# Half of the turned weight rows get their remainder from Pool instead of VectorE

## The reference, cut to what matters

```python
x = fwht(x * SU_ug) / SCALE
x_up = x @ W_up.T * (Wscale_ug[:INTER] * SCALE)
x_gate = x @ W_gate.T * (Wscale_ug[INTER:] * SCALE)
x = jax.nn.silu(x_gate) * x_up
x = fwht(x * SU_dp) / SCALE
x = x @ W_down.T * (Wscale_dp * SCALE)
```

## Time and profile before

| | |
|---|---|
| median of 3 runs | 2642.16 us (2639.2 to 2642.7) |
| the profiled execution | 2643.02 us |
| its span | 2641.2 us, so 1.8 us lie around it |
| PE busy | 2573.5 us (97%) |
| DVE busy | 2243.6 us (85%) |
| POOL busy | 2044.3 us (77%) |
| ACT busy | 1815.0 us (69%) |
| granted PE clock | 0.996 of full speed |

### The profile page before, as it was taken

The page is one execution under the profiler, slowest core; times in us unless marked ns, Lnnn a source line. Parts: engine busy times, 40 slices in busy tenths (PEclk is TensorE's granted clock), DMA queues, the critical chain, the costliest instruction groups (busy, mean ns, idle before and its releaser), DMA issues.

```text
span 2641.2 us, 46296 instructions
## 1 busy us (share of the span) xinstructions
PE 2573.5 (97%) x16048; PEld 2185.7 (83%) x16048; DVE 2243.6 (85%) x2573; ACT 1815.0 (69%) x3935; POOL 2044.3 (77%) x1691
## 2 busy tenths in 40 slices
PE   7999989999999999999999999999999999989998
PEld 6566668989888888989888898988888898978888
DVE  6898998899898888899889889989888989889622
ACT  4776777677777777777777767777777777755322
POOL 6776879788787979888797978888797988876322
PEclk9999999999999999999999999999999999999999
DMA  5664246656666666766666665666666566656675
GB/s 182 211 208 167 101 167 215 228 198 240 212 232 219 216 220 205 238 208 229 222 217 226 211 230 198 240 211 231 221 216 220 202 230 211 232 178 225 245 293 192
DMA packets 165209, 564.41 MB, mean 214 GB/s; under 512 B 17264, under 2 KB 19696, under 8 KB 132976
## 3 DMA queue, kind: packets, MB, share of 16 engines
q1 hardware_dynamic: 164976, 561.44, 61.9%
HBM read 527.30 MB, written 34.08 MB: 213 GB/s over the span
## 4 chain that ended last, share of the span: by engine, by line
PE 78%; DVE 10%; ACT 7%; issue 3%; DMA 1%; POOL 1%; SPq 0%; DVEq 0%; ACTq 0%; POOLq 0%
PE pF L726 21%; PE hT L633 14%; PE pM L651 13%; PE pD L742 10%; PE pM L703 8%; DVE h L1205 5%; DVE acc L1218 3%; PE pM L673 3%; PE pD L766 3%; ACT decay L1011 2%; PE decay L726 2%; PE hT L625 1%; PE pF L766 1%; ACT delta L988 1%; ACT delta L983 1%
## 5 line engine op out<-in xcount | busy, mean ns | idle before, releaser
L1205 DVE TENSOR_TENSOR_SCAN h<-decay,dbx 128x512 f32<-128x512 f32 x1024 | 1200.3, 1207 | 72.6 <-ACT decay L1011 44.0
L1389 POOL TENSOR_TENSOR dbx<-u,bb 128x2048 f32<-128x2048 f32 (+1 forms) x272 | 1179.3, 4336 | 37.4 <-DVE h L1205 35.4
L1011 ACT ACTIVATE decay<-delta,a_neg 128x255 f32<-128x255 f32 x2048 | 873.9, 468 | 300.7 <-DVE h L1205 293.6
L1218 DVE SCALAR_TENSOR_TENSOR acc<-hT,bcT,acc 128x1024 f32<-128x1024 f32 x480 | 610.5, 1272 | 138.5 <-PE hT L633 134.7
L726 PE MATMUL pF<-fxT_hi,wug 128*128 128x256 f32 x3712 | 724.6, 288 | 0.0
L726 PEld LDWEIGHTS pF<-fxT_hi,wug 128*128 128x128 f32 x3712 | 595.4, 192 | 0.2
L633 PEld LDWEIGHTS hT<-ident,h 128*128 128x128 f32 x4096 | 473.1, 141 | 140.0 <-issue 90.0
L633 PE MATMUL hT<-ident,h 128*128 128x128 f32 x4096 | 535.8, 274 | 31.7 <-DVE acc L1218 20.5
L726 PE MATMUL pF<-fxT_lo,wug 128*128 128x256 f32 x1856 | 525.3, 283 | 0.0
L651 PE MATMUL pM<-xnT,w_in 128*128 128x256 f32 x2016 | 480.1, 381 | 3.5 <-ACT hid L931 2.1
L651 PEld LDWEIGHTS pM<-xnT,w_in 128*128 128x128 f32 x2016 | 367.3, 191 | 51.0 <-issue 5.0
(11 more groups left out here) (177 smaller groups left out, 2672.3 us busy)
## 6 DMA issues: line engine op xcount, KB each, us to landing
wug<-scratch_ug SPq DMA_DIRECT2D x243, 1024.0 KB, 4.8
wd<-scratch_wd SPq DMA_DIRECT2D x243, 512.0 KB, 4.1
w_in<-in_W_in SPq DMA_DIRECT2D x252, 256.0 KB, 3.0
bb<-scratch_bc SPq DMA_DIRECT2D x128, 256.0 KB, 4.7
xb<-in_hidden_states SPq DMA_DIRECT2D x16, 512.0 KB, 5.0
xr<-in_hidden_states SPq DMA_DIRECT2D x16, 512.0 KB, 5.9
out<-xr SPq DMA_DIRECT2D x15, 512.0 KB, 3.7
kept_ug<-scratch_ug SPq DMA_DIRECT2D x7, 1024.0 KB, 8.1
```

The lines of the kernel that those rows point to most:

```text
L1011: e = act.activation(da[q % 2][:, i, 1:], delta[c % 2][:, dt, 1:], ACT.Exp, scale=a_neg[:, dt, n:n + 1])
L1205: dve.tensor_tensor_scan(row(h[n % 2][:, tiles, :]), row(da[q % 2][:, :, :]), row(dbx[n % 2][:, tiles, :]), 0.0, ALU.mult, ALU.add).then_i ...
L1218: dve.scalar_tensor_tensor(acc[c % 2][:, tb, :], hT[:, :], cn, acc[c % 2][:, tb, :], ALU.mult, ALU.add).then_inc(acc_done, 1)
L1389: pool.tensor_tensor(dbx[n % 2][:, tiles, :], u[:, tiles, :], rows, ALU.mult).then_inc(done if restarts(c) else prod_done, 1)
```

## The change

Among tiles 4 to 47 those with o modulo 4 of 0 or 2 (22 tiles, `POOL_LO`) no longer have an instruction on DVE. ACT writes, after the rounded part of such a tile, the scaled value in fp32 into the place of the remainder, with a second ACTIVATE from the same bank (semaphore `had_raw`). Pool then subtracts the rounded part in place (`had_difference`, semaphore `had_sub`). The bank is free for PE once ACT has made its second copy. SP stores the lo part after both `had_lo` and `had_sub`. ACT now waits, at a group's first tile, for the store of the set's lo part too. Pool runs the differences of slots k-1 and k in its step of even slot k, behind the product, the convolution additions and most of its other work of the step.

```diff
+        POOL_LO = [o for o in range(KT, NTILE) if o % KT in (0, 2)]
+        DVE_LO = [o for o in range(NTILE) if o not in POOL_LO]
+        def made(table, o):
+            return sum(1 for i in table if i <= o)
+        def first_of(table, g):
+            return next(i for i in table if i // KT == g)
...
             def store_had(g):
                 name, q = GROUPS[g]
-                for s, (part, done) in enumerate((("hi", had_hi), ("lo", had_lo))):
-                    wait_first(sp, done, KT * (g + 1), sp_passed)
+                for s, part in enumerate(("hi", "lo")):
+                    if part == "hi":
+                        wait_first(sp, had_hi, KT * (g + 1), sp_passed)
+                    else:
+                        wait_first(sp, had_lo, made(DVE_LO, KT * g + KT - 1), sp_passed)
+                        if g:
+                            wait_first(sp, had_sub, made(POOL_LO, KT * g + KT - 1), sp_passed)
...
-                    pe.wait_ge(had_lo, NTILE)
+                    pe.wait_ge(had_lo, len(DVE_LO))
+                    pe.wait_ge(had_raw, len(POOL_LO))
...
                     if o >= len(had_bank):
-                        pe.wait_ge(had_lo, o - len(had_bank) + 1)
+                        old = o - len(had_bank)
+                        if old in POOL_LO:
+                            pe.wait_ge(had_raw, made(POOL_LO, old))
+                        else:
+                            pe.wait_ge(had_lo, made(DVE_LO, old))
...
                 if r == 0 and split_use(g):
                     act.wait_ge(had_stored[f"{SETS[g]}_hi"], 16 * split_use(g))
+                    act.wait_ge(had_stored[f"{SETS[g]}_lo"], 16 * split_use(g))
                 act.activation(split_row("hi", o), bank_tiles(o), ACT.Copy, scale=had_scale(o)).then_inc(had_hi, 1)
+                if o in POOL_LO:
+                    act.activation(split_row("lo", o).bitcast(F32), bank_tiles(o), ACT.Copy, scale=had_scale(o)).then_inc(had_raw, 1)
...
             def had_low(o):
                 g, r = divmod(o, KT)
                 dve.wait_ge(had_hi, o + 1)
-                if r == 0 and split_use(g):
+                if o == first_of(DVE_LO, g) and split_use(g):
...
                 for o in HAD_EVAC.get((c, k), ()):
-                    had_low(o)
+                    if o in DVE_LO:
+                        had_low(o)
...
+            def had_difference(o):
+                pool.wait_ge(had_raw, made(POOL_LO, o))
+                pool.tensor_tensor(split_row("lo", o), split_row("lo", o).bitcast(F32), split_row("hi", o).bitcast(F32),
+                                   ALU.subtract).then_inc(had_sub, 1)
...
                 if n == 13 and chunk(c + 2) is not None:
                     moments("x", c + 2)
+                for at in (SLOTS * c + k - 1, SLOTS * c + k):
+                    for o in HAD_EVAC.get(divmod(at, SLOTS), ()):
+                        if o in POOL_LO:
+                            had_difference(o)
                 if n == NST - 1:
```

More of the change, by code:

```diff
@@ L168, in fused_block @@
         had_setup = sem("had_setup"); w_first_in = sem("w_first_in"); diag_done = sem("diag_done"); turned_dve = sem("turned_dve"); turned_pool = sem("turned_pool")
-        had_mm = sem("had_mm"); had_hi = sem("had_hi"); had_lo = sem("had_lo")
+        had_mm = sem("had_mm"); had_hi = sem("had_hi"); had_lo = sem("had_lo"); had_raw = sem("had_raw"); had_sub = sem("had_sub")
         had_stored = {name: sem(f"had_stored_{name}") for name in split}
```

## The result

| | before | after |
|---|---|---|
| median of the runs, us | 2640.76 (2639.03 to 2644.05, 9 runs) | 2649.12 (2645.92 to 2651.73, 9 runs) |
| profiled execution, us (span) | 2643.02 (2641.2) | 2649.12 (2647.3) |

The ratio of the times is 1.0032, with a 95% interval from 1.0021 to 1.0042. The change makes the kernel slower by 8.4 us; 2650.0 had been predicted. The two profiled executions differ by 6.1 us only, since the one of before lies 2.3 us over its median and the one of after on it.

The account below looks back on a forecast made before the run. DVE was taken to bound slots 10 to 16 of turn 0 and turn 1's last third, PE slots 19 to 29. 7.3 + 0.6 + 0.5 = 8.4 us, said as 8: 2642.2 + 8 = 2650 us, range 2642 to 2656.

Parts of the forecast that it names:

- The subtraction: On Pool, 128 x 512 with two SBUF inputs: 1.28 us each, from a line between 256 and 1024 columns.
- Rival 3: Pool's subtractions are slower, sharing something with DVE as in the butterflies: 8.2 us more, 2658 us; chance 0.06.
- Pool's row: From slots 10 to 15, turn 0: Pool chain without holes from 117.2, 42.6 us, last addition ending 159.8, 8.3 later.
- The silu's slack: ACT's silu waits for Pool's last addition with 1.0 us of slack, so slot 19's scan comes 7.3 us later.
- Who passes it on: From slot 20 of turn 0 PE has no slack, is the full engine and can't make up for anything.
- Tile 6 and tile 30: Slots 2 and 27, where PE waits for ACT behind the copy: 0.59 us each, 1.2 us together.
- The store waits: ACT waits for the lo store at groups' first tiles: in time or hidden in turn 0; 0.5 us in turn 1.
- ACT's slot: In slots 10 and 12 to 15 it grows from 4.90 to 5.13 us, 0.23 us longer than DVE's was.
- Rival 2: ACT is the limit and Pool's lateness stays within its products' head start: about +2 us, 2644 us; chance 0.22.
- rival 1: DVE's relief decides, in slots 10 to 15 and late turn 1: 5.5 us less, 2637 us; chance 0.08.

Follow-up runs that it names:

- variant with six tiles: Against the changed kernel, only tiles 12, 14, 16, 18, 20 and 22 go to ACT and Pool, the other 16 stay on DVE; 2646.84 us, 1.0020.
- the first: The changed kernel with tiles 12, 14, 16, 18, 20 and 22 given back to DVE, the other 16 staying on Pool; 2644.09 us, 1.0008.
- third: The changed kernel with Pool's subtractions one step later, right behind that step's product, tile 22's behind the last addition; 2645.16 us, 1.0015.
- fifth: The kernel before plus ACT's 22 copies and its store waits; DVE still makes every remainder, Pool has nothing new; 2646.04 us, 1.0019.
- sixth experiment: The changed kernel with one more Pool subtraction, in a spare buffer, ahead of each of tiles 12 to 22's; 2654.67 us, 1.0054.
- Pool's part alone: The kernel before plus six Pool subtractions on an unread buffer at the places of tiles 12 to 22; 2643.20 us, 1.0011.
- experiment with four tiles: Against the changed kernel, only tiles 14, 42, 43 and 45 go to ACT and Pool; 2641.38 us, 1.0003.

## Why the prediction was right

It gave 2650.0 us and slower with a chance of 0.68; 2649.12 was measured. The mechanism is the one forecast. By its steps:

- **The subtraction**, taken from a line between two forms at 1.28 us: measured 1.27 (1.263 to 1.289, 22 times), beside busy scans. Rival 3, with 2.65 us from the butterflies, is out. Its 2652 ns were a mean of 2.59, 1.13, 4.27 and 2.61 us, and the short one bears the line out, which gives 1.14 us for 448 columns. It began while DVE ran its batch-norm statistics, the other three while DVE ran a TENSOR_TENSOR. Timeline of POOL, before:
```profile
37.08 1.13 POOL L359 TENSOR_TENSOR had_down<-had_pong 128x448 f32<-128x448 f32 x1
```
By the rule cited from the Trainium skill, page "SBUF — State Buffer", section "Who interferes with whom", the 1.27 us were to be expected, and the trace agrees: DVE's scans, accumulations and remainders read one operand from PSUM in this stretch, and the products too keep their 4.55 us.
- **Pool's row**: forecast without a hole from 117.2 to 159.8, measured from 117.04 to 159.08. The row is 0.6 us shorter than the sum, since I added lengths and neighbours overlap a little: the next instruction starts 1.22 us after a subtraction began (128.72 to 129.94) and 4.58 after six additions began (122.91 to 127.49). The last addition is 7.6 us late. The prediction doesn't say where this arises: the product of state 6 starts at 118.41 instead of 111.40, so 7.0 us stand ahead of it, in the wait for tile 12 and its subtraction. The five subtractions behind it add 0.5 us: they fill the holes that the row had before.
- **The silu's slack** is the term that was mis-sized. I took 1.0 us, from Pool's last addition to the start of the table load, and so 7.3 us at slot 19. The load does not wait for the addition: it ran at 155.58, and only the silu behind it waited, 2.25 us. The slack is 1.0 + 1.28 = 2.3 us. With the row's own end it gives 159.08 - 151.53 - 2.3 = 5.3 us, and 5.3 was measured. The variant of a step later confirms it: its last addition is 3.8 us late, its slot 19 only 1.7.
- **Who passes it on**: PE does not catch up, as said. In the variant with six tiles the 4.7 us stand unchanged to slot 66.
- **Tile 6 and tile 30.** The 0.6 of tile 6 is seen in the row's start, 117.04 against 116.42 in the experiment without that copy. The 0.6 at slot 28 appears wherever tile 30 is copied (after, and the first, third, fifth and sixth experiment) and nowhere else. PE's wait there rose from 2.03 to 2.61 us, in the timeline of PE after:
```profile
200.28 1.13 PE L706 MATMUL pM<-dtin,w_dt 128*128 128x256 f32 x4 [2.61 <-ACT delta L1007]
```
- **The store waits.** In turn 1, 2.2 us of waiting for tile 40 were forecast; 2.29 were measured. Tile 36 waits 2.15 us in the same way, which I had not counted; by slot 41 nothing of it is left. From slot 36 to slot 50 the shift grows by 0.6 us, DVE then gains 0.7 by slot 60, and another 0.6 is lost at slot 61, wherever tile 46 is copied: 0.5 in all, as counted. In turn 0 tile 16 waits 1.75 us for its store, which I had counted as in time or hidden: it was late, and hidden. Timeline of ACT, after:
```profile
125.88 0.69 ACT L935 ACTIVATE had_x_hi<-pD,row_scale 128x512 fp32r<-128x512 f32 x1 [1.75 <-DMA scratch_ug<-had_x_lo]
...
293.02 0.69 ACT L935 ACTIVATE had_r_hi<-pD,su_ug 128x512 fp32r<-128x512 f32 x1 [2.29 <-DMA scratch_ug<-had_r_lo]
```
- **ACT's slot**: forecast 5.13 us, measured 4.99 to 5.08 (its decays start at 128.72, 133.71, 138.73 and 143.81). Pool's step of two slots takes 11.7 us (from one copy of the carry at 129.94 to the next at 141.63), so 5.85 a slot: Pool is the limit and not ACT. Rival 2, with ACT as the limit and Pool's lateness absorbed, falls in the dense stretch. There ACT alone gives 0.8 us where that rival counted 1.2, while Pool alone gives 3.2 with shorter subtractions. Over the whole kernel it may have been priced too low: I gave the copies +2 us with the relief, and without the relief they cost 3.5 to 5.3. The copies with the relief but without Pool's part were not run.
- **DVE's relief**, rival 1, is out in the dense stretch, where DVE idles 11.7 us. The rule cited with it from the Trainium skill, page "Perfetto Trace Analysis", section "Identifying the Most-Contended Engine", read as the prediction read it, gave the wrong sign for this change: DVE was the busiest engine of the stretch, and moving work off it onto ACT and Pool made the stretch 5.5 us longer. A relief of DVE without that load elsewhere was not run in this stretch.

The sum, then: 5.3 at slot 19, 0.6 at slot 28 and 0.5 in turn 1 are 6.4 us, where the forecast had 8.4 with its 7.3. The spans of the two traces are 6.1 apart, and the clock moves them both ways (last section). Before's trace has a fall of the clock at slot 28 that after's has not: between slots 29 and 36 the shift goes from 5.9 to 4.4. After's in turn has more of the lower clock around slot 64: between slots 64 and 67 its shift goes from 4.9 to 6.2. The two about cancel, which leaves the 6.4. The medians say 8.4, with an interval of 5.5 to 11.1 us. So the direction and the mechanism are shown, but that 8 us agree with 8.4 is partly luck, since one term was 2.0 us too large. The 2 us by which the medians exceed the sum stay open. A candidate that the sum leaves out is the 1.4 us at slots 64 to 67.

## What to carry to other kernels

Work may be moved off the busiest engine only onto one that has room in the same stretch: add up the receiver's holes up to the next thing that others need from it, here 6.2 us of holes for 7.6 us of work, with a silu at the end. But this difference is not the forecast. By it the last addition would have come 1.4 us late, less than the silu's slack of 2.3. It came 7.6 us late, since the first moved instruction waited 4.74 us with a product queued behind it, and still 3.8 us late without that wait. So where the moved instruction stands in the receiver's queue counts as much as its length: the same instructions one step later, behind the product instead of ahead of it, cost 3.9 us instead of 8.4. And in these traces the table load ran ahead of the wait of its ACTIVATE (load at 155.58, silu at 159.11), so the slack of a producer is counted to the ACTIVATE and not to the load.

## What the runs showed of the chip that I had not expected

**The clock falls after PE's short waits, in some executions and not in others.** At slot 27 and 28 PE waits 2.0 to 2.6 us for `delta`. Busy time with granted clock, before from 189 to 199 us, and after at the same place, from 195 to 205:
```profile
189.00:199.00 10.00, 7.97 (x23) 4.07 (x22) 7.53 (x8) 7.73 (x14) 4.68 (x2) 0.84 0.60 210
```
```profile
195.00:205.00 10.00, 7.39 (x33) 4.53 (x32) 6.26 (x7) 8.14 (x14) 5.92 (x3) 1.00 0.58 209
```
The mean of 0.84 lies between the two levels, 1.2 and 2.4 GHz: part of the stretch ran at the lower. After waited longer, 2.61 us against 2.03, and kept the full clock; the variant with six tiles waited 2.04 and fell to 0.83, and the one with Pool's part alone waited 2.04 and kept 1.00. The four matmuls behind it took 2.99 us in the first of these two, from its timeline of PE:
```profile
201.51 2.99 PE L787 MATMUL pD<-had_in,h_minus 128*128 128x512 f32 x4
```
and 1.88 in the second:
```profile
199.41 1.88 PE L766 MATMUL pD<-had_in,h_minus 128*128 128x512 f32 x4
```
In the latter the shift against before falls by 1.6 us between slots 29 and 32. Around 355 us it is the same. Busy time with granted clock from 355 to 371 us, in before and in after:
```profile
355.00:371.00 16.00, 12.28 (x71) 9.73 (x70) 13.17 (x13) 10.55 (x23) 12.45 (x8) 0.96 0.83 296
```
```profile
355.00:371.00 16.00, 10.41 (x50) 8.77 (x51) 13.54 (x13) 10.99 (x25) 10.14 (x7) 0.76 0.90 306
```
The experiment with six tiles had 0.89 there, and the one with four 0.77. Between slots 64 and 66 the experiment with four tiles lost 2.3 us, more than the change had brought, and between slots 64 and 67 after lost 1.4. With ACT's part alone it was 0.9, and there twelve matmuls that took 2.76 us before took 4.38, in its timeline of PE:
```profile
360.48 4.38 PE L653 MATMUL pM<-xnT,w_in 128*128 128x256 f32 x12
```
All six traces in which tiles of turn 1 are copied by ACT lose 0.8 to 2.5 us here, and the two without (the experiments with six tiles and with Pool's part alone) lose nothing, though they meet the lower clock too. So this loss may belong to the change, by putting the fall where PE has more to do; no run was made that shows it. What decides whether an execution meets the fall I can't tell from these runs. It makes a single trace uncertain by 1 to 2.5 us, as much as the smaller terms here, so only medians of many runs decide, and shifts in a trace are to be read between places with the same clock.

**Pool's subtraction of a buffer from itself is faster**: 1.04 us for 128 x 512 where two different inputs take 1.27. Whether one input read twice or the output's type (f32 and not fp32r) does it was not separated. A stand-in for a cost should have the operands of the real one.
